# Two-layer graph kernel: x turned by VectorE and on-chip transfers, masked exponentials in place, and new orders

## What is computed

```python
u = einsum('bnh,bmh->bnm', x, x) / sqrt(128)
delta = softmax(u) * adj
att = delta / (sum(delta, axis=2) + 1e-10)
# parts of att right of, on and left of the diagonal meet three projections of x
ctx = att_left @ (x @ Wl.T + bl) + att_self @ (x @ Ws.T + bs) + att_right @ (x @ Wr.T + br)
x = layernorm(x + relu(ln_w * normalised(ctx) + ln_b))
# second layer
d = (sum(adj, axis=-1) + 1e-05) ** -0.5
x = layernorm(x + (d[:, None] * adj * d[None, :]) @ (x @ weight) + bias)
```

## Time and profile before

| | |
|---|---|
| median of three runs | 464.2 us (464.04 to 466.09) |
| the profiled execution: its time | 465.88 us |
| the profiled execution: its span | 464.2 us |
| busy: PE, DVE, ACT, POOL | 449.6, 385.9, 296.0, 296.0 us |
| moved by the transfers | 76.72 MB |

### The profile page before, as it was taken

How to read it: one execution, slowest core, us unless ns; L and a number is a source line. 1 busy time by engine, 2 the same in 40 slices (tenths; PEclk the granted TensorE clock), 3 DMA queues, 4 the chain that set the end, 5 groups by cost and what they waited for, 6 DMA issues and landing times. The chain is left out here.

```text
span 464.2 us, 8778 instructions
## 1 busy us (share of the span) xinstructions
PE 449.6 (97%) x2711; PEld 364.3 (78%) x2711; DVE 385.9 (83%) x678; ACT 296.0 (64%) x611; POOL 296.0 (64%) x364
## 2 busy tenths in 40 slices
PE   7999999999999999999999999999999999999793
PEld 4799987697967978599776997769886798877562
DVE  3989998898878898788888988789897887998705
ACT  2867787785574876566685765658558676757410
POOL 2324766678655867468663875739665578678762
PEclk9999999999999999999999999999999999999988
DMA  7654739695860897418981289804997066377701
GB/s 174 244 179 114 209 80 241 189 237 141 250 227 1 197 272 208 142 45 195 271 236 73 72 200 270 277 1 108 256 222 234 0 165 200 72 188 172 183 23 45
DMA packets 64269, 76.72 MB, mean 165 GB/s; under 512 B 5696, under 2 KB 56000, under 8 KB 64224
## 3 DMA queue, kind: packets, MB, share of 16 engines
q1 hardware_dynamic: 64160, 76.11, 61.2%
q0 software_dynamic: 64, 0.07, 0.1%
HBM read 38.40 MB, written 4.19 MB: 92 GB/s over the span
## 5 line engine op out<-in xcount | busy, mean ns | idle before, releaser
L783 ACT ACTIVATE e_rows<-ps_u,nmax 128x1024 f32<-128x1024 f32 x62 | 69.0, 1113 | 69.9 <-DVE nmax L1036 69.6
L449 PE MATMUL ps_c<-h_sum,dT 128*128 128x128 f32 x896 | 110.4, 275 | 0.0
L1373 POOL TENSOR_TENSOR dM<-dT,parts 128x384 f32<-128x384 f32 x64 | 68.4, 1068 | 64.9 <-ACT dT L790 55.8
L449 PEld LDWEIGHTS ps_c<-h_sum,dT 128*128 128x128 f32 x896 | 107.0, 192 | 2.5 <-issue 1.4
L469 PE MATMUL ps_y<-aT,x1p 128*128 128x512 f32 x224 | 101.7, 592 | 0.0
L1036 DVE TENSOR_REDUCE nmax<-ps_u 128x1 f32<-128x1024 f32 x62 | 75.5, 1217 | 22.7 <-PE ps_u L376 22.2
L1044 DVE CUSTOM_DVE_ANT_0 d_rows<-e_rows,a_rows 128x1024 f32<-128x1024 f32 x64 | 84.9, 1327 | 7.8 <-PE ps_d L434 7.7
L790 ACT ACTIVATE dT<-ps_d 128x1024 f32<-128x1024 f32 x64 | 65.2, 1018 | 27.7 <-PE ps_d L434 21.3
L1051 DVE STREAM_TRANSPOSE a_blk<-a_rows 128x1024 f32<-128x1024 f32 x64 | 77.9, 1230 | 0.0
L469 PEld LDWEIGHTS ps_y<-aT,x1p 128*128 128x128 f32 x224 | 40.8, 190 | 37.8 <-issue 37.3
L434 PE MATMUL ps_d<-parts,d_rows 128*128 128x128 f32 x512 | 66.8, 273 | 1.4 <-DVE dsum L1044 1.2
(11 more groups left out here) (92 smaller groups left out, 710.7 us busy)
## 6 DMA issues: line engine op xcount, KB each, us to landing
a_rows<-in_adj_dram SPq DMA_DIRECT2D x64, 512.0 KB, 5.2
aT<-a_blk SPq DMA_DIRECT2D x224, 128.0 KB, 2.4
x_rows<-in_x_dram SPq DMA_DIRECT2D x8, 512.0 KB, 5.1
a_rows<-a_blk SPq DMA_DIRECT2D x32, 128.0 KB, 2.4
out_dram<-fin SPq DMA_DIRECT2D x15, 256.0 KB, 2.7
out_dram<-fin SPq DMA_DIRECT2D x2, 128.0 KB, 1.8
wraw<-in_L_gnn_Wl_dram SPq DMA_DIRECT2D x1, 64.0 KB, 3.4
wraw<-in_L_gnn_Wr_dram SPq DMA_DIRECT2D x1, 64.0 KB, 3.1
```

Of the source, the lines that this page charges most:

```text
L449: pe.matmul(ps_c[:, c_place(b, i), :], dT[:, i % 2, j, :], h_sum[:, b % 2, j, k * H:(k + 1) * H], start=t == 0, stop=False)
L783: act.activation(e_rows[:, i % 2, :], u_bank(b, i), ACT.Exp, bias=nmax[:, i % 2:i % 2 + 1], accum_out=zsum[:, i:i + 1]).then_inc(exp_done, 1)
L1373: pool.tensor_tensor(dM[:, i % 2, :, :], dT[:, i % 2, i, :].rearrange("p (a c) -> p a c", a=1).to_broadcast([P, 3, P]), parts[:, :, :], AL ...
```

## The change

It has four parts.

1. **x of batches 1 to 7 is turned without PE.** `turn_rows(b)` on DVE transposes the 32 x 32 squares of x of batch b + 1 into `x_blk`; `move_rows(b)` on SP brings them to their partitions (`x_turned`) with 16 transfers of 32 KB. `x_high` then waits for all of these and reads SBUF instead of PSUM, and `x_low` does so too, in two pieces of 256 columns per half instead of one of 512. The columns of a half are now interleaved over all blocks, so `project` of these batches waits for both halves. Batch 0 is turned by PE as before.
2. **Masked exponentials in place.** `e_rows` is gone; `d_rows` is a ring of three, into which `exps` writes and in which `masked` works in place. `exps` waits for the `turn_d` of three blocks earlier, and `masked` no longer waits for PE.
3. **The weights** are loaded into a part of `fin`, and the first warming matmul pair is 128 columns shorter.
4. **All lists are written anew.** In the middle batches the scores of block 7 belong to their own batch now; loads, copies and stores change places too.

```diff
@@ SBUF
+        x_blk = sb("x_blk", [P, NQ, NB, Q])
+        x_turned = sb("x_turned", [P, NQ, NB, Q])
-        e_rows = sb("e_rows", [P, 2, N])
-        d_rows = sb("d_rows", [P, 2, N])
+        d_rows = sb("d_rows", [P, 3, N])
@@ sync
+            def move_rows(b):
+                sp.wait_ge(rows_turned, b + 1)
+                if b > 0:
+                    sp.wait_ge(xt_split, 2 * (b + 1))
+                for q in range(NQ):
+                    for m in range(NQ):
+                        sp.dma_start(x_turned[m * Q:(m + 1) * Q, q, :, :], x_blk[q * Q:(q + 1) * Q, m, :, :])\
+                          .then_inc(rows_moved, 16)
@@ tensor, first_products
-                for c in (slice(0, HALF), slice(HALF, N)):
+                for c in (slice(0, HALF), slice(HALF, HALF + 3 * P)):
@@ tensor, project
-                pe.wait_ge(xt_split, 2 * b + j // HB + 1)
+                pe.wait_ge(xt_split, j // HB + 1 if b == 0 else 2 * b + 2)
@@ scalar, x_high
-                act.wait_ge(xt_tr, 2 * b + k + 1)
+                if b == 0:
+                    act.wait_ge(xt_tr, k + 1)
+                else:
+                    act.wait_ge(rows_moved, ROW_MOVES * b)
@@ scalar, exps
-                wait(act, d_ready, g - 1)
+                wait(act, dt_tr, g - 2)
...
-                act.activation(e_rows[:, i % 2, :], u_bank(b, i), ACT.Exp, bias=nmax[:, i % 2:i % 2 + 1],
+                act.activation(d_rows[:, g % 3, :], u_bank(b, i), ACT.Exp, bias=nmax[:, i % 2:i % 2 + 1],
@@ vector, x_low
+                for lo, hi, v in zip(x_pieces(x_half(xT_lo, b, k), b), x_pieces(x_half(xT_hi, b, k), b),
+                                     x_pieces(x_columns(b, k), b)):
+                    last = dve.scalar_tensor_tensor(out=lo, in0=v, scalar=SHRINK, in1=f(hi), op0=ALU.mult,
+                                                    op1=ALU.subtract)
+                last.then_inc(xt_split, 1)
@@ vector, masked
-                wait(dve, dt_tr, g - 1)
-                dve.tensor_tensor_reduce(out=d_rows[:, i % 2, :], in0=e_rows[:, i % 2, :],
+                dve.tensor_tensor_reduce(out=d_rows[:, g % 3, :], in0=d_rows[:, g % 3, :],
@@ vector
+            def turn_rows(b):
+                dve.wait_ge(x_in[(b + 1) % 2], 16 * ((b + 1) // 2 + 1))
+                wait(dve, rows_moved, ROW_MOVES * b)
+                dve.transpose(x_blk[:, :, :, :],
+                              x_rows[:, (b + 1) % 2, :, :].rearrange("p i (m c) -> p m i c", m=NQ, c=Q))\
+                   .then_inc(rows_turned, 1)
@@ sync, first_batches(b, p)
                 load_biases()
+                next_x(p)
                 load_a(p, 0)
-                next_x(p)
                 load_a(p, 1)
                 load_norm_constants()
+                move_rows(p)
                 load_a(p, 2)
```

More of the change, by code:

```diff
@@ new lines, in batch @@
+                gather(p, 0, HB, 4, 8)
+                scores(b, 7)
+                gather(p, HB, NB, 0, 4)
+                m_read_h(b, 7)
+                second_product(p, 0, HB)
+                gather(p, HB, NB, 4, 8)
+                turn_d(b, 5)
+                m_read_o(p, 0, HB)
+                second_product(p, HB, NB)
+                context_far(b, 4)
+                context_near(b, 4)
+                turn_d(b, 6)
+                context_far(b, 5)
+                context_near(b, 5)
@@ new lines, in first_batches, with batch @@
+                diagonal(b, 2)
+                diagonal(b, 3)
+                exps(b, 6)
+                d_out(b, 4)
+                degree(b, 4)
+                y_out(p, 0, HB)
+                degree(b, 5)
+                exps(b, 7)
+                norm_c(b, 0, HB)
+                d_out(b, 5)
+                diagonal(b, 4)
+                degree(b, 6)
+                y_out(p, HB, NB)
+                degree(b, 7)
+            def batch(b, p):
+                x_high(b, 0)
+                diagonal(p, 5)
+                d_out(p, 6)
+                x_high(b, 1)
+                norm_x(p, 0, HB)
+                degree(b, 0)
@@ L1209, in first_batches @@
                 stats_f(p, 0, HB)
-                turn_blocks(b, 3)
+                masked(b, 7)
                 turn_blocks(b, 4)
-                turn_blocks(b, 5)
-                masked(b, 6)
+                stats_x(b, 0, HB)
                 add_out(p, HB, NB)
@@ L1231, in batch @@
                 add_bias(b, 2)
-                stats_x(p, 0, HB)
                 row_max(b, 1)
+                turn_blocks(p, 7)
                 add_bias(b, 3)
-                turn_blocks(p, 7)
+                masked(b, 1)
+                row_max(b, 2)
                 add_bias(b, 4)
@@ L1274, in last_batches @@
                 add_bias(b, 0)
-                row_max(b, 0)
+                masked(b, 1)
+                stats_x(p, HB, NB)
+                row_max(b, 3)
                 add_bias(b, 1)
-                masked(p, 7)
+                masked(b, 2)
+                row_max(b, 4)
+                turn_blocks(b, 0)
+                masked(b, 3)
+                add_out(p, 0, HB)
+                row_sums(b, 0)
                 add_bias(b, 2)
-                masked(b, 0)
-                row_max(b, 1)
@@ L1519, in last_batches @@
[L1519 to L1549 removed]
+                self_term(b, HB, NB - 2)
```

876 lines of the change are left out of this document (421 added, 455 removed).

## The result

The change makes the kernel slower: 487.7 us (median of 4 runs, 486.5 to 490.5) against 465.1 us for the kernel before in the same comparison; the ratio is 1.049 (95% interval 1.046 to 1.053). I had forecast 466.8 with a range of 460 to 472: the right side, and far too small.

The account below looks back on a forecast made before the run. PE was taken to bound the whole middle. From 464.2: -6.0 transposes, -1.2 waits, -0.4 end, +9.8 start, +0.4 small new waits, giving 466.8 us, range 460.0 to 472.0.

Parts of the forecast that it names:

- SP has room: SP's queue in a middle batch: its copies, loads and stores take 34 us of 55, so the copies of x are hidden.
- The transposes, -6.0: PE, batches 1 to 7: 56 transposes of x at 0.107 us each leave, 6.0 us less.
- The copies at the start: Start: batch 1's x_high waits for 16 copies landing at 22.8, delaying exps(2) to 25.7 and PE's scores of block 4.
- I take 0.5 us, between them: SP's issue cost per 32 KB copy of x, put at 0.5 us, between bounds of 0.39 and 0.65.
- my walk: Start, three lists stepped through: scores of block 4 at 25.7, work up to 31.7 instead of 22.82, 8.9 us late.
- so I take half of it, 0.9: Start, PE's clock after waiting 2.2 us for exps(2): half of the 1.7 us cost of half speed, 0.9.
- its end (-0.4 forecast: End of the last batch: one more piece of gather covers the last read-out, 0.4 us less.
- The waits of rows 3, -1.2: PE's few waits for masked between the two ends: the third buffer takes them away, 1.2 us less.
- The masked product keeps its size in place: DVE's masked product: working in place does not change its size.
- become the bound in the middle: Rival, middle batches: waits for DVE make a batch 55.2 instead of 54.6, total 470.4 us; chance 0.12, within the likeliest case.
- the start costs more than it gives: Rival, start: lateness over 9.5 us outweighs the gains, 464.8 to 471 us; likeliest, chance 0.48.
- D: How late the start makes PE: forecast 9.8 us, up to 13 with slowest issue and whole clock loss; the rest comes to -7.2.

Follow-up runs that it names:

- e12: The change with each copy of x cut from 32 KB to 4 KB, the rest of x_turned zeros: 484.8 us, ratio 1.044.
- e6: The change with batch 1's x turned by PE and the earlier kernel's order until scores of block 3 of batch 1, batch 2's x loaded earlier: 477.0 us.
- e1: The change with x_high and x_low of batch 1 moved later in the start's ACT and DVE lists: 481.1 us, ratio 1.033.
- e9: e6 with the earlier order up to scores of block 5 of batch 1, turn_rows right behind row_max of block 5, and e8's last batch: 465.9 us.
- e3: The change with batch 2's x loaded ahead of the 16 copies of batch 0's second half of adj: 485.3 us, ratio 1.042.
- e4: The change with the last batch in the middle batches' order up to the scores of block 6: 480.6 us, ratio 1.032.
- e8: e7 with the last batch of e4, its masked product of block 5 ahead of a turn_blocks: 470.0 us, ratio 1.010.
- e5: The kernel before with only the ring of three buffers and the masked product in place: 464.8 us, ratio 0.999.
- e7: e6 with the 16 copies of batch 2's x issued by POOL in two groups instead of SP: 481.3 us, ratio 1.033.
- e10: The change with scaling by lnw and shift by lnb cut to one column of 128: 484.5 us, ratio 1.043.

## Why the prediction was right in sign and wrong in size

The change took 20.9 us more than forecast. 5.4 of it are at the start, which the forecast walked and sized too small; 12 are at two places which it put at nothing: the hand-over from batch 1 to batch 2, covered by "SP has room", and the middle of the last batch, not walked. So the sign was right for the reason given, the start, but most of the slowdown was not foreseen; with the start sized right the same sum would have been 472.2.

**The transposes, -6.0: right.** The work of PE fell by 6.1, and a middle batch is 0.9 us shorter.

**The copies at the start: right in mechanism, too small.** The step that failed is "I take 0.5 us, between them, because the copies are of the same kind as the latter but carry a quarter of it". The issue costs 0.635 whatever is carried (e12), so the 16th copy is issued 2.0 us later than forecast; the first started 0.3 late, and the last landed at 25.0 instead of 22.8. PE came back 2.1 later than in my walk (27.82, not 25.7). "The idle stretch is shorter than the only one shown, so I take half of it, 0.9" failed too: I counted 2.2 us of waiting and it was 5.37, since the copies were 2 us later and PE had run out of work 1 us sooner. Nor is the whole of it 1.7: scores and `turn_d` are 1.4 + 0.85 in the same walk, so at half speed they take 2.25 more. Measured are 2.5, with a `project`, 1.6 more than I took. With these, 9.8 becomes 13.5; measured are 13.7 at the scores of block 5, which is where my walk ends. The second slow stretch behind it, 1.5 us, I did not have at all. e6, with the lists of before at the start and batch 1's x turned by PE, loses 7.5 us at 40: so the 15.2 belong to the copies and the new lists there, though how they divide between the two is from the walk and from e1, and not from a run for each.

**"SP has room": wrong as a sum over a batch.** 34 of 55 us is true of a middle batch, and there no copy is waited for. At the change from batch 1 to batch 2 three groups of 16 and a load stand in a row behind a late `turn_blocks`, and 5.6 us go (0.3 before). e9 takes the wait away with batch 1 undelayed and `turn_rows` early. e3 shows that it is not enough to move the load.

**The last batch: not walked.** I compared only its end (-0.4 forecast; there the loss went from 13.1 to 13.3, about even). In the middle of it 6.8 us went by the order of the lists alone (e4, e8). No row of before could have shown it; the two lists did, and the chain of 4.8 us per block could have been added up from the earlier trace rows and the timeline.

**The waits of rows 3, -1.2.** They are gone in the change, but not by the third buffer, as I had it: with the buffer alone they stay (e5). That leaves the new order; no run has it alone.

**"The masked product keeps its size in place": right about the place (1325 ns), wrong about this kernel (1447).** The new order puts it beside POOL's products.

**Rivals.** DVE did not become the bound in the middle. That the start costs more than it gives was the likeliest and came true past its bounds: D is 13.7 at the end of the walk and 15.2 at 40 us, where the forecast had at most 13; and two more places lost nearly as much again. Of the signs named, `x_high` had 7.99 us of idle ACT before it (forecast 6), and the third `exps` came at 26.48 (24.5). In sum, on the profiled spans, which differ by 21.3: the 2.6 forecast, 5.4 more for the start, 5.3 and 6.7 for the two other places beyond what the kernel before loses there, and 0.6 between 40 and 100 us, make 20.6; the remaining 0.7 are in the small terms. The medians differ by 22.6, since the profiled execution of the kernel before lay 0.8 over the median of this comparison (465.88 against 465.1) and that of the change 0.5 under its own.

## What to carry to other kernels

When a change comes with new orders, walk every list of it once, the first, the middle and the last batch, and at each handing-on of batches add up what stands in one queue; a mean load over a batch hides a line of three groups. Work that is taken off the bounding engine is worth its time only if the thing put in its place is early enough: copies within the chip cost by their number, here 0.635 us each, so that a turn by 16 copies needs 11.5 us of lead and is worthless where there is none, as for batch 1. Repair place by place and count where PE does no work: the last repair of such a chain decides whether the whole is faster or slower.

## What the runs showed of the hardware

- SP's queue issues a copy inside SBUF every 0.635 us, be it of 4, 32 or 128 KB (10.12, 10.13 and 10.34 us for 16); some groups of 128 KB took up to 12.0 us. POOL's queue issued the copies of 32 KB every 0.50 us (e7), and both queues worked at once; POOL itself stood still meanwhile.
- The masked product (two inputs in SBUF, 1.22 us alone) took 2.29 us beside POOL's products of two inputs, and POOL's next one 2.07 instead of 1.3.
- After 5.37 us without work PE did its next 5.4 us of work at 1.2 GHz, and after 3.03 us without work it was slow too; even two waits of 0.65 and 0.80 us were followed by such a stretch, of some 3 us. In the four kernels with the same start (the change, e3, e4, e10) the loss of the first 40 us came out between 20.6 and 22.3 us.
